# Sixteen-expert stage: slot rows that carry their pick's number, and outputs scattered to picks inside the loop

## The reference, cut to what matters

```
def moe_ffn(x2d, w_router, w_gate_up, w_down):
    logits = x2d @ w_router
    probs = jax.nn.softmax(logits, axis=-1)
    vals, idx = jax.lax.top_k(probs, TOPK)                 # TOPK = 2 of E = 16
    vals = vals / jnp.sum(vals, axis=-1, keepdims=True)
    combine = jnp.sum(jax.nn.one_hot(idx, E) * vals[..., None], axis=1)
    for e in range(E):
        gate, up = jnp.split(x2d @ w_gate_up[e], 2, axis=-1)
        h = jax.nn.silu(gate) * up
        out = out + combine[:, e:e + 1] * (h @ w_down[e])
```

## Time and profile before

| what | value |
|---|---|
| runs | 1339.92, 1345.71, 1343.07 us; median 1343.07 us |
| profiled execution | 1343.59 us, its span 1341.8 us |
| PE busy | 1196.5 us (89% of the span), fillers among them |
| DVE, ACT, POOL busy | 585.3, 391.9, 85.5 us |
| chain that ended last, by line | L1972 5%, L1989 2%, L1863 1%, L1871 1% |

### The profile page before, as it was taken

The page is one execution under the profiler, slowest core; times in us unless marked ns, Lnnn a source line. Parts: engine busy times, 40 slices in busy tenths (PEclk is TensorE's granted clock), DMA queues, the critical chain, the costliest instruction groups (busy, mean ns, idle before and its releaser), DMA issues. The chain is left out here.

```text
span 1341.8 us, 26884 instructions
## 1 busy us (share of the span) xinstructions
PE 1196.5 (89%) x9992; PEld 855.6 (64%) x9993; DVE 585.3 (44%) x1737; ACT 391.9 (29%) x939; POOL 85.5 (6%) x128
## 2 busy tenths in 40 slices
PE   0999999998987999998998899989989989889993
PEld 0677677665564667666577677766755666657772
DVE  5272345415352557576574022215742762512223
ACT  2123312322313545342340133312421531012220
POOL 2000000000000000000001300022000000040004
PEclk9999999999999999999998899999989999889997
DMA  8200000000000000490004111117400000021113
GB/s 229 72 3 3 0 2 3 1 2 2 1 2 1 1 1 2 89 265 1 1 1 109 54 48 49 50 42 186 130 1 0 1 1 1 25 75 48 49 44 108
DMA packets 32146, 57.25 MB, mean 43 GB/s; under 512 B 3557, under 2 KB 28870, under 8 KB 31018
## 3 DMA queue, kind: packets, MB, share of 16 engines
q1 hardware_dynamic: 28856, 48.47, 13.4%
q0 software_dynamic: 3072, 6.30, 1.6%
q10 hardware_dynamic: 114, 1.04, 0.3%
HBM read 41.83 MB, written 13.86 MB: 42 GB/s over the span
## 5 line engine op out<-in xcount | busy, mean ns | idle before, releaser
L192 PE MATMUL banks<-mask,ident 128*128 128x256 bf16 x1346 | 171.1, 287 | 19.0 <-PEq L88 14.6
L1972 PE MATMUL banks<-gu,sxT 96*128 x496 | 173.5, 493 | 1.2 <-ACT sxT L2008 1.0
L192 PEld LDWEIGHTS banks<-mask,ident 128*128 128x128 bf16 x1346 | 136.1, 103 | 49.0 <-issue 26.0
L2034 DVE TENSOR_TENSOR h<-sg,banks 128x384 f32<-128x384 f32 x62 | 34.4, 554 | 236.5 <-ACT sg L2016 236.5
L226 PE MATMUL banks<-xT,weights 96*96 96x512 f32 (+3 forms) x288 | 131.9, 604 | 2.5 <-ACT xT L1524 1.5
L1356 ACT ACTIVATE work<-banks,nmax 128x128 f32<-128x128 f32 (+1 forms) x288 | 104.4, 417 | 97.5 <-DVE nmax L1395 97.5
L1972 PEld LDWEIGHTS banks<-gu,sxT 96*128 96x128 f32 x496 | 90.8, 193 | 52.6 <-issue 4.2
L1395 DVE TENSOR_REDUCE nmax<-banks 128x2 f32<-128x256 f32 (+1 forms) x144 | 79.9, 555 | 53.5 <-PE banks L1293 49.6
L226 PEld LDWEIGHTS banks<-xT,weights 96*96 96x96 f32 (+3 forms) x288 | 48.3, 174 | 65.0 <-issue 58.0
L1268 PE MATMUL banks<-K,Q 96*128 96x128 f32 (+1 forms) x384 | 78.6, 328 | 5.0 <-PEq L88 5.0
L702 ACT ACTIVATE work<-banks 98x1024 f32<-98x1024 f32 (+1 forms) x48 | 49.1, 1023 | 110.4 <-PE banks L569 110.4
(11 more groups left out here) (255 smaller groups left out, 1623.5 us busy)
## 6 DMA issues: line engine op xcount, KB each, us to landing
gu<-in_L2f_gu SPq DMA_DIRECT2D x1, 6912.0 KB, 37.4
xin<-slots_in SPq DMA_DIRECT2D x62, 96.0 KB, 1.9
slots_out<-y SPq DMA_DIRECT2D x62, 96.0 KB, 1.6
gu<-in_L3f_gu SPq DMA_DIRECT2D x1, 5184.0 KB, 29.0
dn<-in_L2f_dn SPq DMA_DIRECT2D x1, 4608.0 KB, 47.6
slots_in<-zeros SPq DMA_DIRECT2D x1, 2976.0 KB, 22.5
dn<-in_L3f_dn SPq DMA_DIRECT2D x1, 2592.0 KB, 34.5
gu<-in_L2f_gu SPq DMA_DIRECT2D x1, 2304.0 KB, 12.9
```

The lines of the kernel that those rows point to most:

```text
L192: nc.tensor.matmul(env.banks[:, bank, first:first + 2 * P], env.ident16[:, :], env.mask16[:, :, :], start=True, stop=True)
L1972: ins = nc.tensor.matmul(banks[:, 2 + 2 * par + n, 0:EF], w.sxT[:, par, k, :], w.gu[:, bass.ds(e, 1), k, n * EF:(n + 1) * EF].rearrange("p ...
```

## The change

For the sixteen-expert stage alone:

- There is a new DRAM tensor `slots_own` of 193 numbers a row. Its last column carries the number of the pick whose row it is. `pick_ids` holds, for each token row and each of its two picks, `a * 128 + p`; `spare_ids` holds for every slot a number past the picks, for slots that stay empty. VectorE makes both in `first_loads`; SyncE clears `slots_own` and writes the spare numbers to its last column in `relative_setup`.
- `M` gets a 193rd column. `route` puts the numbers of the first picks there. `sort_tokens` scatters the first picks of all 8 tiles, then for each half renames the column to the second picks and scatters those.
- In `experts` ScalarE loads the last column of `slots_own` into `ids` at the start. SyncE only loads tiles; GpSimd scatters each output tile by its `ids` column to `picks_out`, in which picks lie in order and spare rows behind them. Its code is written out 31 times.
- `causal_setup` loads `picks_out` with four plain transfers of SyncE, and TensorE runs 130 fillers instead of 240.

```diff
@@ first_loads
-            dve.wait_ge(cast, 3)
+            rows = env.small["rows"]
+            nc.vector.tensor_scalar(env.pick_ids[:, :, :].rearrange("p t k -> p (t k)"), env.iota[:, 0:PICKS], float(P),
+                                    rows[:, 0:1], ALU.mult, ALU.add).then_inc(cast, 1)
+            nc.vector.tensor_scalar(env.spare_ids[:, :], env.iota[:, 0:SLOT_TILES], float(P),
+                                    rows[:, 1:2], ALU.mult, ALU.add).then_inc(cast, 1)
+            dve.wait_ge(cast, 5)
@@ relative_setup
+            own = env.slots_own.rearrange("(t p) c -> p t c", p=P)
+            sp.dma_start(own[:, :, 0:C], env.zeros[:, None, :].to_broadcast([P, SLOT_TILES, C])).then_inc(env.slots_zeroed, 16)
+            sp.dma_start(own[:, :, C:C + 1], env.spare_ids[:, :, None].bitcast(F32),
+                         allow_slow_non_contiguous=True).then_inc(env.slots_zeroed, 16)
@@ causal_setup
                 for q in range(TILES // 2):
-                    sp.wait_ge(gathered[q], 64)
+                    src = env.picks_out[q * 4 * P:(q + 1) * 4 * P, :].rearrange("(a p) c -> p a c", p=P)
+                    sp.dma_start(before.picked_y[:, 4 * q:4 * q + 4, :], src).then_inc(gathered[q], 16)
+                for q in range(TILES // 2):
+                    sp.wait_ge(gathered[q], 16)
...
-            fill(nc, env, 14 if before is None else 240, 0)
+            fill(nc, env, 14 if before is None else 130, 0)
...
-            if before is not None:
-                gather(nc, env, before, gathered)
@@ route
-            nc.gpsimd.tensor_copy(w.M[:, span(ip * PT, PT), :], xn[:, :, :]).then_inc(kept, 1)
-            pool.wait_ge(kept, 1)
+            nc.gpsimd.tensor_copy(w.M[:, span(ip * PT, PT), 0:C], xn[:, :, :]).then_inc(kept, 1)
+            if first:
+                own_ids(nc, env, w, kept, span(ip * PT, PT), 0)
+            pool.wait_ge(kept, 2 if first else 1)
@@ sort_tokens
-                pool.wait_ge(env.slots_zeroed, 16)
+                pool.wait_ge(env.slots_zeroed, 48)
                 pool.wait_ge(slots_ready, 1)
-                scatter(nc, env, w, scattered)
-                pool.wait_ge(scattered, 16 * PICKS)
+                for t in range(TILES):
+                    scatter_own(nc, env, w, t, 0, first_picks[t // PT])
+                for half in range(2):
+                    pool.wait_ge(first_picks[half], 16 * PT)
+                    own_ids(nc, env, w, renamed, span(half * PT, PT), 1)
+                    pool.wait_ge(renamed, half + 1)
+                    for t in range(half * PT, half * PT + PT):
+                        scatter_own(nc, env, w, t, 1, second_picks)
+                pool.wait_ge(second_picks, 16 * TILES)
@@
+def own_ids(nc, env, w, sem, tiles, k):
+    nc.gpsimd.tensor_copy(w.M[:, tiles, C:C + 1].bitcast(I32), env.pick_ids[:, tiles, k:k + 1]).then_inc(sem, 1)
+
+def scatter_own(nc, env, w, t, k, sem):
+    a = 2 * t + k
+    nc.gpsimd.indirect_dma_start(
+        env.slots_own[:, :], bass.IndirectOffsetOnAxis(ap=w.slot_index[:, a:a + 1], axis=0),
+        w.M[:, t, :], None).then_inc(sem, 16)
@@ combine
-    dve.wait_ge(gathered[q], 64)
+    dve.wait_ge(gathered[q], 64 if w.shared else 16)
@@ experts
+        slots = env.slots_in if w.shared else env.slots_own[:, 0:C]
...
-                sp.dma_start(w.xin[:, par, :], rows(env.slots_in, i)).then_inc(x_loaded[par], 16)
+                sp.dma_start(w.xin[:, par, :], rows(slots, i)).then_inc(x_loaded[par], 16)
...
-            pipeline(sp, SLOT_TILES, ((load, 0), (store, 5)))
-            sp.wait_ge(y_stored[0], 16 * ((SLOT_TILES + 1) // 2))
-            sp.wait_ge(y_stored[1], 16 * (SLOT_TILES // 2))
+            pipeline(sp, SLOT_TILES, ((load, 0), (store, 5)) if w.shared else ((load, 0),))
...
+            if not w.shared:
+                ids = env.slots_own[:, C:C + 1].rearrange("(t p) c -> p t c", p=P)
+                nc.scalar.dma_start(w.ids[:, :, None], ids, allow_slow_non_contiguous=True).then_inc(ids_loaded, 16)
             load_function(nc, env, ACT.Silu)
...
+            else:
+                pool.wait_ge(ids_loaded, 16)
+                for i in range(SLOT_TILES):
+                    pool.wait_ge(y_out, i + 2)
+                    nc.gpsimd.indirect_dma_start(
+                        env.picks_out[:, :], bass.IndirectOffsetOnAxis(ap=w.ids[:, i:i + 1].bitcast(U32), axis=0),
+                        w.y[:, i % 2, :], None).then_inc(y_stored[i % 2], 16)
+                pool.wait_ge(y_stored[0], 16 * ((SLOT_TILES + 1) // 2))
+                pool.wait_ge(y_stored[1], 16 * (SLOT_TILES // 2))
```

## The result

The changed kernel takes **1356.09 us** (median of 20 runs, 1348.46 to 1370.78), the kernel before, measured beside it again, 1344.40 us (20 runs, 1339.92 to 1362.97). The ratio is **1.0072 with an interval of 1.0052 to 1.0093**: slower by 0.7%, where 1336.5 us (1332.5 to 1342) was forecast. Ratios and intervals here leave out the few runs in a slower state, and so aren't the quotients of the medians. The profiled execution of the changed kernel has a span of 1356.6 us, the one of before 1341.8.

A forecast was written before the change was run, and what follows sets the result against it. It took GpSimd's scatters to bound the sort, TensorE the expert loop, and filler, with gathers close behind, the set-up; 0.3 + 0.8 + 0 + 2.5 - 10.2 = -6.6 gave 1336.5 us (1332.5 to 1342).

The forecast's parts named there:

- the clearing at the start: Second stage: 3968 more rows and a column of 3968 pieces, 8.9 us each, queue empty near 59; cost 0.
- The slower rival: Start: 4-byte writes on SyncE's queue delay first attention's small transfers; at 200 ns each 1357 us; chance 5%.
- (a): First stage: two more small VectorE operations behind L272, hidden by nothing, +0.3 us.
- (b): Sort: two renamings of the last column by GpSimd copies between scatters, 0.4 us each, +0.8 us.
- (c): Start of the expert loop: ScalarE's load of the last column beside the first tile, hidden by filler matmuls, 0 us.
- The column in front of the tile: Loop start: ScalarE's column pieces all go first, first tile slips 7.2 us beyond cover, 1343.7 us; chance 8%.
- (d): End of the expert loop: GpSimd's last scatter, its wake and an extra barrier lengthen the hand-over, +2.5 us.
- The cheap hand-over: Loop end: GpSimd closes the stage as SyncE does, costing 1.2 us, time 1335.2 us; chance 10%.
- (e): Set-up of the next attention: four plain SyncE loads replace 16 gathers, first landing after 3.1 us, -10.2 us.
- GpSimd didn't slow the loop: Denies a rival: in the expert loop GpSimd's scatters hold up VectorE, 0.3 us a tile, 1345.8 us; chance 5%.

The follow-up runs named there:

- the kernel with the late transfers: The changed kernel with SyncE issuing the two transfers into slots_own at the start of the first attention, not ending the second stage: 1343.49 us, ratio 1.0000.

## Why the prediction was wrong, step by step

**The step that failed: the clearing at the start, costed at 0.** The prediction asked when the queue would be empty, and was right in sum: near 59, landed at 58.8, and the first small transfer of the attention comes 49.7 us after that stage's start, before 49.0. It didn't ask what the *issue* costs SyncE. It has no term for that. The old clearing's issue had taken 0.43 us, on a queue with room, and SyncE has to reach the stage's barrier behind its last issue. The measured price is 18.4 us. The nearest row was in the page of before: 22.5 us from issue to landing of one clearing. A bound "SyncE is held for as long as the transfer ahead moves" would have been an upper end that holds.

**The slower rival had the place and not the price.** It named the 4-byte writes on SyncE's queue at the start. Most of those pieces took 9 ns on an engine, and 9 to 28 on average in six of the profiles, less than the 36 ns of the big ones and never near its 117. Nor is it so that the trace of before has no piece so small: it has 3558 packets of 4 bytes, 9 ns each in the median. The mechanism that it missed made the same place cost nearly what it gave (1357 against 1356.09), by chance.

**(a) First stage, +0.3: right.** From L272's start to the next stage 12.87 - 11.41 = 1.46 us, before 13.27 - 12.10 = 1.17.

**(b) Sort, +0.8: near, +0.6.** A renaming widens the gap between two scatters from 1.27 to 762.89 - 761.45 = 1.44 us, twice, less than half of the 0.4 that was taken. Another 0.14 is the last landing, 2.47 us after its issue instead of 2.33.

**(c) Start of the loop, 0: right in time, wrong in kind.** The first output comes 0.16 us later. The first tile lands 0.9 us later, inside the cover, and the column at 776.68 + 4.6 = 781.3, 5 us into the stage and not 12. But the cover was thinner than it looked: the second tile landed 4.7 us into the stage instead of 3.05, and in the kernels whose sort closed 0.7 us sooner the clock stayed low there for up to 7 us more. The column in front of the tile, a rival at 7.2 us, didn't happen.

**(d) End of the loop, +2.5: under-sized, +3.55.** GpSimd's wake took 0.28 us (0.5 was taken), the extra barrier 0.5 (as taken). What failed is to take the end of the sort for its price: the sort closes behind 16 scatters with a drain of 1.36 us, the loop behind 31 with 2.58. The cheap hand-over is refuted: even where SyncE does the waiting the difference is 2.1. By the first-byte latencies that the Trainium skill gives ("DMA: Bandwidth & Descriptors", Specifications) an estimate for it is 0.4; the rows don't agree.

**(e) Set-up, -10.2: over-sized, -8.3.** All but one term came out: adding 1.55 a load, 7.90 us of normalising (8.24 taken), a hand-over of 0.97, filler hidden. The first load landed 5.35 us after the filler's start, not 3.2, and its other end, 4.7, was too near as well. In nine profiles of kernels with these loads it came 3.6 to 6.6 us after the issue, in six of them 5 us or more. Why is not settled: SyncE's third issue was held 2.73 us in one profile and 0.50 in another, with landings at 5.4 us in both, so that isn't it.

**Not in the sum: the clock behind it.** The fill ended 4.75 us before the stage, and the projection lost 1.3 us to half clock; the feed-forward after it gained 3.4 us, since its half clock of before is gone. The latter is 36.93 us in all nine kernels with the short set-up and 38.6 to 40.3 in the five with the long one, with the same instructions.

Put together, 0.3 + 0.6 + 0.2 + 3.5 - 8.3 + 1.3 - 3.4 = -5.8 without the clearing, which agrees with the -6.0 us in the stages of the kernel with the late transfers, and +12.6 with it; the medians differ by 11.7, and 0.7% are 9.7. The rest of the forecast, 6.6 us faster, was nearly right in sum, by errors that cancel. GpSimd didn't slow the loop: from the first to the last output are 119.17 us, before 119.18. That is 3.97 us a tile, where the prediction read 4.45 from the whole stage.

## What to carry to other kernels

Give every issue two prices: when its transfer lands, and for how long the issuing engine stands there; behind a transfer of 3968 pieces the second was 16.6 to 20.0 us here, on an empty queue 0.42 to 0.46, and what stands behind the engine, a barrier above all, pays it. A transfer behind one so large belongs at a place where its engine has nothing to do next (here the head of a long stage), or on another engine's queue. Where GpSimd takes over the last store of a stage, add its drain, which grew with the number of its transfers (1.36 us after 16, 2.58 after 31), and let another engine wait for the landing, which saved about half of it here.

## What the runs showed of the hardware that was not expected

- A transfer's issue on SyncE was held for 16.6 to 20.0 us behind one of 3968 pieces and let go with 965 to 1665 of these left, alike for 1024 or 3968 new pieces and for 4 or 768 bytes a piece. Another engine's queue with 3785 pieces to go held nothing (0.44 us).
- Writing a piece of 4 bytes took 9 ns on a DMA engine in most cases, 9 to 28 on average.
- GpSimd's drain at a barrier took 1.35 to 1.36 us after 16 indirect transfers that had landed and 2.58 after 31. Begun before the last landing, it ended 0.70 us (16) and 1.31 us (31) behind it.
- The same kernel's runs spread from 1332 to 1352 us with a mean granted clock from 0.975 to 0.959, through stretches at half clock in a stage that no edit touched. Stage lengths of the profiles told the edits apart where the medians couldn't.
